# Deformable sampling in a convolution chain: three of nine taps by dense weights instead of two

## The reference

```
off = conv3x3(h, off_w) + off_b          # 2 groups x 9 taps x (dy, dx), and 18 masks
py  = off_y + row + ky;   px = off_x + column + kx
v   = bilinear sample of h at (py, px), for each of 2 channel groups and 9 taps, 0 outside the image
g   = v * sigmoid(mask)
out = sum over channels and taps of dc_w * g      # then batch norm, leaky relu, 1x1 conv, batch norm, leaky relu, + x
```

## Time and profile before

| | us |
|---|---|
| median of 3 runs | 4013.23 (4012.5 to 4016.01) |
| profiled execution: span on the core | 4500.8 |
| in it, first gather issued | 2854.4 |
| busy over the span: PE, DVE, ACT, POOL | 3405.0, 3169.4, 2843.2, 907.3 |

### The profile page before, as it was taken

One profiled execution on the slowest core, in us unless ns is written; L12 is line 12 of the kernel. 1 busy time (PEld: TensorE's weight loads), 2 busy tenths in 40 slices (PEclk: granted clock), 3 DMA queues, 4 the chain that ended last, 5 costly groups with the idle time before them and its releaser, 6 DMA issues. The chain is left out here.

```text
span 4500.8 us, 58636 instructions
## 1 busy us (share of the span) xinstructions
PE 3405.0 (76%) x22186; PEld 1347.4 (30%) x22186; DVE 3169.4 (70%) x3652; ACT 2843.2 (63%) x2698; POOL 907.3 (20%) x974
## 2 busy tenths in 40 slices
PE   3777559999999999999999998447556655674445
PEld 2454333233333333333334343112112212221111
DVE  5999768999999984999999994234435444444445
ACT  1444326999999994999999992234434444443444
POOL 2000010000000000000000000445554554545452
PEclk7656569999999999999999998757767777776667
DMA  2200000000000000000000000211211111121110
GB/s 43 89 1 1 1 3 1 1 1 1 1 1 2 2 1 1 1 1 1 1 1 2 2 1 13 52 34 38 54 41 38 47 46 33 43 54 39 39 41 21
DMA packets 117631, 89.65 MB, mean 20 GB/s; under 512 B 96496, under 2 KB 98576, under 8 KB 117340
## 3 DMA queue, kind: packets, MB, share of 16 engines
q0 software_dynamic: 28672, 58.78, 4.7%
q1 hardware_dynamic: 87036, 26.32, 2.6%
q10 hardware_dynamic: 1632, 0.56, 0.1%
HBM read 65.61 MB, written 19.96 MB: 19 GB/s over the span
## 5 line engine op out<-in xcount | busy, mean ns | idle before, releaser
L1556 ACT ACTIVATE adder_layer_Z<-adder_layer_CP,AN 128x2048 f32 x984 | 1873.3, 2013 | 33.4 <-PE PS L1517 32.6
L1517 PE MATMUL PS<-adder_layer_Z,c_adder_out 128*32 128x512 f32 x16896 | 1845.0, 593 | 57.9 <-ACT adder_layer_Z L1556 33.1
L1602 DVE TENSOR_SCALAR adder_layer_Z<-adder_layer_CP,AW 128x2048 f32 x1128 | 1369.9, 1281 | 45.5 <-PE PS L1517 31.5
L1517 PEld LDWEIGHTS PS<-adder_layer_Z,c_adder_out 128*32 128x32 f32 x16896 | 649.6, 110 | 1253.0 <-issue 1176.1
L1973 POOL DMA_INDIRECT sampler_G<-neighbours,sampler_IDX x896 | 849.6, 948 | 834.9 <-DVEq L2039 436.9
L2260 ACT ACTIVATE sampler_HY<-PS,G_hat 128x512 f32<-128x512 f32 x512 | 309.0, 686 | 319.6 <-PE PS L2139 119.6
L1609 DVE SCALAR_TENSOR_TENSOR adder_layer_Z<-adder_layer_CP,AW,adder_layer_Z 128x1024 f32<-128x1024 f32 x384 | 476.4, 1282 | 35.6 <-issue 35.6
L2148 PE MATMUL PS<-sampler_HXM,G_spread 32*128 32x512 f32 x128 | 99.1, 864 | 387.4 <-DVEq L2065 341.9
L2063 DVE TENSOR_TENSOR P<-sampler_HY,PS 128x2048 f32<-128x2048 f32 x64 | 146.4, 2287 | 338.9 <-remote 255.3
L2262 ACT ACTIVATE sampler_HY<-sampler_HY 128x2048 f32<-128x2048 f32 x128 | 244.6, 1911 | 8.7
L1474 POOL MEMSET XP<- 128x4624 f32 x1 | 4.0, 3952 | 1046.4 <-PE PS L1533 1046.4
(11 more groups left out here) (376 smaller groups left out, 3018.8 us busy)
## 6 DMA issues: line engine op xcount, KB each, us to landing
sampler_G<-neighbours,sampler_IDX POOLq DMA_INDIRECT x896
neighbours<-top_k_zero SPq DMA_DIRECT2D x16, 578.0 KB, 7.2
neighbours<-sampler_HT SPq DMA_DIRECT2D x256, 32.0 KB, 1.7
X<-in_x SPq DMA_DIRECT2D x8, 256.0 KB, 6.3
out<-X SPq DMA_DIRECT2D x8, 256.0 KB
P<-in_L_conv_conv_w SPq DMA_DIRECT2D x4, 144.0 KB
P<-in_L_conv_add_w SPq DMA_DIRECT2D x4, 144.0 KB
RAW<-in_L_conv_w SPq DMA_DIRECT2D x4, 144.0 KB
```

What stands on the lines that cost most here:

```text
L1517: mm = t.matmul(PS[32 * j:32 * j + 32, k, :], K["adder_out"][:, 32 * i:32 * i + 32], Z[:, r % SLOTS, j, c:c + BANK], start=False, stop=Fal ...
L1556: op = a.activation(z(r, j), seen(ch, ty, tx), ACT.Relu, bias=ANf[:, weight(ty, tx, j, i)])
L1602: op = v.tensor_scalar(z(r, j), seen(ch, ty, taps[0]), AWf[:, weight(ty, taps[0], j, i)], 0.0, ALU.subtract, ALU.max)
```

## The change

- Six taps are gathered, three are dense: 12 gathers a step, and 96 units instead of 64. An odd step has two units, an even one has one (`units`). In an odd step VectorE multiplies its first unit right behind sample(n) and its second at the end of the step; TensorE spreads the second unit and contracts the first in between. The masks for four units come three times in eight steps, before twice.
- ScalarE's pass max(0, 1 - distance) is gone. VectorE takes min(distance, 1) and multiplies by the x hat in the pass that it makes anyway; the x hat is spread with the factor -1. So the product is -min(distance, 1) times the x hat, which is the hat's product less the x hat itself. What is missing, the sum over rows of the image times the x hat, is added by TensorE: once an image, eight matmuls make the column sums HS (stage 5), and each contraction begins with one matmul of HS with the x hat (32 partitions, 32 columns, 512 pixels).
- The values of 12 gathers fill three chunks of 128 rows instead of three and a half. The dense values get three buffers, their weight product is a call of its own (`deform_dense`), and the closing passes move two steps back (LAST, OUTER, FINAL).

The core of the diff:

```diff
-NTAP = 7
+NTAP = 6
+NCHUNK = GK * CG // 128
+NUNIT = NB * HALVES * DG * NDENSE * PX // BANK
-    c["spread"] = (p[:, None] % 32 == p[None] % 32) * 1.0
+    c["spread"] = (p[:, None] % 32 == p[None] % 32) * -1.0
...
-                    t.wait_ge(h_t, b + 1)
+                    if k == 0:
+                        t.wait_ge(h_t, 2 * b + 1)
+                        for tl in range(TILES):
+                            mm = t.matmul(PS[:, 7, 0:128], GR["spread"][:, :], HT[:, b % 2, tl, :], start=(tl == 0),
+                                          stop=(tl == TILES - 1))
+                        mm.then_inc(h_t_ps, 1)
+                    else:
+                        t.wait_ge(h_t, 2 * b + 2)
...
+                    if k == 0:
+                        a.wait_ge(h_t_ps, 2 * b + 2)
+                        a.activation(HS[:, b % 2, :], PS[:, 7, 0:128], ACT.Copy, scale=-1.0).then_inc(h_t, 1)
...
-                g = {1: 2 * (n // 8) + 1, 5: 2 * (n // 8) + 2}.get(n % 8)
+                g = {1: 3 * (n // 8) + 1, 3: 3 * (n // 8) + 2, 6: 3 * (n // 8) + 3}.get(n % 8)
...
+            def units(n):
+                return ([3 * (n // 2) + 1, 3 * (n // 2) + 2] if n % 2 else [3 * (n // 2)]) if 0 <= n < NT else []
...
-                            v.tensor_tensor(M[part][:, :, :], HY[:, part],
-                                            HXB.unsqueeze(1).broadcast_to([128, HATS, BANK]), ALU.mult)
+                            v.scalar_tensor_tensor(out=M[part][:, :, :], in0=HY[:, part], scalar=1.0,
+                                                   in1=HXB.unsqueeze(1).broadcast_to([128, HATS, BANK]),
+                                                   op0=ALU.min, op1=ALU.mult)
...
                             sample(n)
+                            for w in units(n)[:-1]:
+                                mix(w)
                             if n and prepared(n - 1) is not None:
                                 mask_hats(prepared(n - 1))
                             next_stage(v, stage_dve, n, 1)
-                            mix(n)
+                            mix(units(n)[-1])
...
+                        t.matmul(PS[0:32, 5, :], HS[32 * e:32 * e + 32, b % 2, ch],
+                                 HXM[32 * e:32 * e + 32, w // 4 % 2, :], start=True, stop=False, skip_group_check=True)
                         for part in range(2):
...
                             turn_values(n)
-                        if 0 < n <= NT:
-                            contract(n - 1)
+                        for w in units(n - 1)[-1:]:
+                            contract(w)
+                        for w in units(n)[1:]:
+                            spread(w)
+                            contract(w - 1)
...
-                        if n + 1 < NT:
-                            spread_y(n + 1)
-                            spread_x(n + 1)
+                        for w in units(n + 1)[:1]:
+                            spread(w)
...
                                 a.activation(HY[:, part, j, :], PYB, ACT.Abs, bias=GR["hat"][:, c:c + 1])
-                            a.drain()
-                            a.activation(HY[:, part].rearrange("p c f -> p (c f)"),
-                                         HY[:, part].rearrange("p c f -> p (c f)"), ACT.Relu, scale=-1.0, bias=1.0)\
-                             .then_inc(hy, 1)
+                            a.drain().then_inc(hy, 1)
```

More of the change, by code:

```diff
@@ L1795, in stage_act @@
                 elif s == 4:
-                    a.wait_ge(h_t_ps, b + 1)
+                    a.wait_ge(h_t_ps, 2 * b + 1)
                     if b >= 2:
@@ L1895, in weights_pe @@
                     t.transpose(PS[:, 5, 64:128], rawcv, K["ident"][0:64, 0:64])
[L1896 to L1899, removed]
+                    for c in range(NCHUNK):
+                        t.transpose(PS[:, 5, 128 + 64 * c:192 + 64 * c],
+                                    dcs.rearrange("o g c -> o (g c)")[:, 128 * c:128 * c + 128], K["ident"][0:64, 0:64])
                     for c in range(NDENSE * DG):
@@ L1941, in prepared, with unit @@
             def prepared(n):
-                g = {1: 2 * (n // 8) + 1, 5: 2 * (n // 8) + 2}.get(n % 8)
[L1944 to L1949, removed]
+                g = {1: 3 * (n // 8) + 1, 3: 3 * (n // 8) + 2, 6: 3 * (n // 8) + 3}.get(n % 8)
+                return g if g is not None and 4 * g < NUNIT else None
+            def units(n):
+                return ([3 * (n // 2) + 1, 3 * (n // 2) + 2] if n % 2 else [3 * (n // 2)]) if 0 <= n < NT else []
+            def unit(w):
+                per_image = NUNIT // NB
+                b, u = w // per_image, w % per_image
+                k, ti, e = u // (4 * NDENSE), u // 4 % NDENSE, u % 4
                 return b, k, ti, e // DG, e % DG
@@ L2163, in deform, with deform_dense @@
                         t.wait_ge(t_sb, th + 1)
-                        for c in range(4):
-                            n = min(128, GK * CG - 128 * c)
+                        for c in range(NCHUNK):
                             t.matmul(PS[64 * h:64 * h + 64, 1, 128 * (tl % 4):128 * (tl % 4) + 128],
-                                     DC[0:n, c, :], VT[0:n, th % (LAG + 1), c, :], start=False, stop=False,
+                                     DC[:, c, :], VT[:, th % (LAG + 1), c, :], start=False, stop=False,
                                      skip_group_check=True)
-                        b, k, ti, h, d = unit(th)
-                        t.wait_ge(v_sb, th + 1)
-                        mm = t.matmul(PS[64 * h:64 * h + 64, 1, :], DCD[:, NDENSE * d + ti, :], VD[th % 2][:, :],
-                                      start=False, stop=(th % per_bank == per_bank - 1), skip_group_check=True)
-                        if th % per_bank == per_bank - 1:
+                    def deform_dense(w):
+                        b, k, ti, h, d = unit(w)
+                        last = w % (NUNIT // (NT // per_bank)) == NUNIT // (NT // per_bank) - 1
+                        t.wait_ge(v_sb, w + 1)
+                        mm = t.matmul(PS[64 * h:64 * h + 64, 1, :], DCD[:, NDENSE * d + ti, :], VD[w % 3][:, :],
+                                      start=False, stop=last, skip_group_check=True)
+                        if last:
                             mm.then_inc(d_ps, 1)
@@ L2203, in _ @@
                     prepare_mask(0)
-                    spread_y(0)
-                    spread_x(0)
+                    spread(0)
                     for n in range(NT + LAST - per_bank + 1):
@@ L2225, in _ @@
                             deform(n - LAG)
+                        for w in units(n - 2)[-1:] if n % 2 else units(n - 2) + units(n - 1)[:1]:
+                            deform_dense(w)
                 @blk.scalar
@@ L2290, in _ @@
                             sample(n)
-                        if 0 < n <= NT:
-                            dense_values(n - 1)
+                        for w in units(n - 1)[-1:]:
+                            dense_values(w)
+                        for w in units(n)[1:]:
+                            hats(w)
+                            dense_values(w - 1)
                         if due(n, BLOCK) is not None:
@@ L2299, in _ @@
                         next_stage(a, stage_act, n, 1)
-                        if n + 1 < NT:
-                            hats(n + 1)
+                        for w in units(n + 1)[:1]:
+                            hats(w)
         phase(sampler)
```

93 lines of the change are left out of this document (46 added, 47 removed).

## The result

The changed kernel takes 4325.43 us (median of 4 runs, 4312.59 to 4330.54) against 4014.62 for the kernel before on the same chip: 1.0768 times as long, 95% interval 1.0751 to 1.0785. That is 311 us slower; the prediction said 191 slower.

A forecast was written before the change was run, and what follows sets the result against it. Gathers were taken to pace the kernel before, the VectorE-TensorE loop the one after. Start 2870.8, plus 1309 for loop pairs, side work and clock, 15.5 for the end and 8.8 carried along gave 4204 us; range 3960 to 4330, the forecast's own 4130 to 4330.

The forecast's parts named there:

- The rebuilt 4004 us: Kernel before: timed run rebuilt from gathers at 1.2514 us each plus the end as profiled, 4004.4 us against 4013 measured.
- The bound changes to the loop of VectorE and TensorE: Sampler after the change: the closed loop of both engines sets the pace, and gathers run ahead with full buffers.
- the 33.1 of the sum: Loop of an odd and an even step after the change: 33.1 us, against 30.0 of gathers now and 35.0 before.
- Rival A: Sampler: the gathers still pace it, faster; 3861 us if every pair stays under 30.0 us; chance 19%.
- rival C: Sampler: the first profile's stalls are in the timed runs also, so the old loop gave 4013; about 4450 us; 6%.
- Durations of the instructions: VectorE in the sampler: multiply 1.73 us, reduce 2.80, one-pass product 2.29.
- Column sum, 0.88 us a unit: TensorE ahead of each contraction: one added serial matmul, taken as 0.88 us, between 0 and 1.97.
- Rival B: TensorE: the loop binds but column sums overlap, 84 us less, 4120 us, near 4040 with side work half hidden; 14%.
- The middle wait of 3.31 us: Odd step between its two products: VectorE waits 3.31 us for spread, column sum and contraction.
- Side work, 68 us an image with preparation: Convolutions, masks, positions, stages waiting across engines and last passes now show: 68 us for each image preparing the next.
- Clock, 27 us: Spread at TensorE's lower clock: 1.6 us a pair in the 17 pairs without convolutions, 27 us, range 0 to 82.
- Stalls by an unknown releaser again: Sign expected in the profile after: waits on a releaser the profile does not know, 508 us in the first profile.

## Why the prediction was right, and where its terms were off

The direction and the mechanism were right: the gathers give up the pace and the loop of VectorE and TensorE takes it. The size was not: 311 us against 191. The measured 4325 us lies 5 us inside the forecast's end at 4330, whose width was drawn for the clock and for the stages that wait on each other; half of the miss came through the column sum. That the time stayed inside is in part luck.

- **What bounds the kernel before**: right. The rebuilt 4004 us against 4013 was read correctly; the second profile and the halved gathers show it.
- **The bound changes to the loop of VectorE and TensorE**: right. Halving the gathers gives back 11 us, and a step's last gather is issued 50 to 85 us ahead of the step's multiply from the seventh step on. Of the signs named, the pairs of the last image, which have no convolution, take 38.5 to 43.5 us, all over the 33.1 of the sum. Rival A (the gathers still pace it) and rival C have fallen.
- **Durations of the instructions** (multiply, reduce, one-pass product): right within 0.03 us.
- **Column sum, 0.88 us a unit**: too small. It is 1.50 by leaving it out, and 0.97 or 1.84 in the timeline by the level of the clock. 96 x 0.62 = 60 us of the miss of 121. The upper bound of 1.97 held.
- **Rival B, the column sums overlap**: wrong for the shape used, where they never do; and the 128-row shape shows that the price I gave the overlap, 0.88 a unit, was wrong as well: it saves 0.11 to 0.13 us up to the next product, because one column group still has both.
- **The middle wait of 3.31 us**: its parts and order are right, its size is the one of the upper clock, and it was not met once: 3.98 us at the least, 4.77 and 6.09 in the two steps shown of the last image, and 6.09 in five of that image's eight odd steps.
- **Side work, 68 us an image with preparation**: too small. With the column sums out of the kernel and of the sum (8 x 30.46 + 68 = 312), these images should take 312 us, or 317 with the clock's share for three of their pairs; without column sums they took 335.9, 336.8 and 335.3, 19 to 20 more each, 58 in all. With the 60 us of the column sum that is nearly all of the 121. Of the 58 the stage of ScalarE is the part that I had left out: VectorE's quantising waits for a stage that ScalarE issues behind the second unit's distances. Moving it gave back 30 us, 10 an image. In the prediction ScalarE "gives nothing back by itself"; its queue order did take something. The other 9 to 10 us an image I have not split: longer waits for masks (8.3 us each where I had put 2.8 us of delay) and the lower clock in loop pieces are in it.
- **Clock, 27 us**: its bound for the odd step's middle was right, 2.8 us: the wait of 6.09 is 2.78 above 3.31. The part of it that was taken was too small, 1.6 us a pair and in 17 pairs only, where the middle alone took the full 2.78 in five of the last image's eight. The lower level acts not on the spread alone, which the prediction names, but on the column sum and the contraction too, and part of the column sum's 60 us is its doing. What it costs over the whole kernel no run shows; idle matmuls in the last image gave back some 10 us.
- **"Stalls by an unknown releaser again"**: wrong. The second profile of the kernel before has none either. I had tied them to the kernel; they belong to one execution.

## What to carry to other kernels

When an instruction queue that paces a kernel is relieved by moving work to other engines, add up the closed loop that takes over, with every order-bound wait in it, before counting what the old bound gives back: here the gathers' pace fell by 160 us, and the kernel became 311 us slower. An added matmul in a waiting chain is not priced by its columns but by its place and by the clock level that it meets: the same one cost 1.50 us a unit ahead of the contraction and 0.61 behind it ((4239.38 - 4181.0) / 96). And each engine that serves a loop in order is part of it: look for what stands ahead of the awaited instruction in the queue of its producer, and for work that fills a wait, which cost 111 us when it was moved behind the wait.

## What the runs showed of the hardware that was not expected

- One profiled execution had 508 us of stalls without a known releaser and a span of 4500.8 us; the next profile of the same kernel had none, 4013.8 us. Here the span beside the timed median of 4013 told the two apart.
- A 32-row matmul in the first of four column groups, ahead of 128-row ones in all four, runs alone: the others start 0.97 us later at the upper clock and 1.84 at the lower; with 128 rows three groups start 0.02 us later, although the matmul then reads four times as many rows.
- Eight idle matmuls between two spreads brought an image's granted clock from 0.76 to 0.82 and its length from 301 to 291 us.
